# Adapter and gate weights beside base_w in one split moving operand, with products of 264 and 384 columns a tile

## What is computed

```
# L0 condition: a 32x32 channel mixer per sample, from 8 attended kernels
att = softmax(gelu(gelu(cond @ W0 + b0) @ W1 + b1) @ W2 + b2)
y   = einsum('boi,bih->boh', einsum('bk,koi->boi', att, weight), x) + (att @ bias_k)[..., None]
# L0 ffn: base layer, and the best 2 of 8 experts of rank 16
w    = top-2 softmax over e of (y @ gate_w.T)
x1   = x + y @ base_w.T + base_b + 2 * sum_e w_e * (y @ lora_A[e].T) @ lora_B[e].T
# L1: a 9-tap grouped convolution over h plus a context, then the best 2 of 4 experts
z    = conv1d(x1, 9 taps, 4 groups) + cond @ c_weight.T + fside
out  = x1 + 4 * (top-2 softmax of z @ router_w.T) over e of (z @ A[e].T) @ B[e].T
```

## Time and profile before

| what | value |
|---|---|
| three runs, median | 185.46 us |
| the profiled execution | 185.67 us |
| its span | 183.7 us |
| PE busy | 176.0 us (96%) |
| PEld busy | 160.1 us (87%) |
| DVE busy | 119.6 us (65%) |
| POOL busy | 84.2 us (46%) |
| ACT busy | 82.9 us (45%) |
| share of the chain that ended last | PE 76%, DVE 16%, ACT 4%, issue 2% |

### The profile page before, as it was taken

One profiled execution on the slowest core, in us unless ns is written; L12 is line 12 of the kernel. 1 busy time (PEld: TensorE's weight loads), 2 busy tenths in 40 slices (PEclk: granted clock), 3 DMA queues, 4 the chain that ended last, 5 costly groups with the idle time before them and its releaser, 6 DMA issues.

```text
span 183.7 us, 3003 instructions
## 1 busy us (share of the span) xinstructions
PE 176.0 (96%) x1087; PEld 160.1 (87%) x1087; DVE 119.6 (65%) x255; ACT 82.9 (45%) x183; POOL 84.2 (46%) x86
## 2 busy tenths in 40 slices
PE   7999999899999999999999999999999999988990
PEld 7998889788888999998889999988889999987970
DVE  1269795987996343987954336987756733577473
ACT  3656759538336066423442267316134652244010
POOL 8023609980396469930009099530007873433000
PEclk9999999999999999999999999999999999999999
DMA  5999000033000410000032000000140000000336
GB/s 176 312 373 366 11 0 2 4 109 121 0 0 25 149 60 0 4 0 0 0 133 99 0 2 0 4 0 0 61 167 4 2 0 4 0 0 2 114 114 228
DMA packets 6350, 12.15 MB, mean 66 GB/s; under 512 B 704, under 2 KB 1088, under 8 KB 6336
## 3 DMA queue, kind: packets, MB, share of 16 engines
q1 hardware_dynamic: 6192, 11.84, 18.1%
q10 hardware_dynamic: 144, 0.13, 0.3%
HBM read 7.77 MB, written 4.19 MB: 65 GB/s over the span
## 4 chain that ended last, share of the span: by engine, by line
PE 76%; DVE 16%; ACT 4%; issue 2%; DVEq 0%; POOL 0%; POOLq 0%
PE ps L895 17%; PE ps L897 17%; PE ps L896 17%; PE ps L917 6%; PE ps L971 5%; PE ps L888 3%; DVE xs L732 2%; DVE late L642 2%; DVE xsl L634 2%; PE ps L932 2%; DVE above L638 1%; PE ps L968 1%; PE ps L1060 1%; DVE outb L720 1%; PE ps L1079 1%
## 5 line engine op out<-in xcount | busy, mean ns | idle before, releaser
L895 PE MATMUL ps<-base_h,xTh 128*128 128x512 f32 x64 | 26.0, 406 | 0.0
L897 PE MATMUL ps<-base_h,xTl 128*128 128x512 f32 x64 | 25.2, 394 | 0.0
L896 PE MATMUL ps<-base_l,xTh 128*128 128x512 f32 x64 | 25.2, 394 | 0.0
L320 POOL TENSOR_TENSOR xTl<-xT_s,xTh 128x512 fp32r<-128x512 f32 x12 | 15.0, 1278 | 15.9 <-ACT xTh L404 15.9
L325 POOL TENSOR_TENSOR zl<-outb,zh 128x340 fp32r<-128x340 f32 x15 | 14.6, 976 | 13.4 <-ACT zh L429 13.3
L336 POOL TENSOR_TENSOR x1Tl<-x1T,x1Th 128x512 fp32r<-128x512 f32 x12 | 16.4, 1379 | 8.1 <-DVE lw L662 8.1
L691 DVE TENSOR_TENSOR outb<-ps,s_sb 128x340 f32<-128x340 f32 x16 | 8.2, 511 | 17.6 <-PE ps L897 11.2
L678 DVE SCALAR_TENSOR_TENSOR x1T<-ps,side_s,xT_s 128x512 f32<-128x512 f32 x16 | 12.0, 749 | 11.3 <-PE ps L897 11.3
L971 PEld LDWEIGHTS ps<-mixT,p 128*128 128x128 f32 x128 | 17.0, 191 | 1.4
L971 PE MATMUL ps<-mixT,p 128*128 128x128 f32 x128 | 17.0, 276 | 0.0
L429 ACT ACTIVATE zh<-outb 128x340 fp32r<-128x340 f32 x16 | 7.8, 489 | 17.9 <-DVE outb L691 13.2
(11 more groups left out here) (183 smaller groups left out, 471.5 us busy)
## 6 DMA issues: line engine op xcount, KB each, us to landing
xT_s<-in_xT_dram SPq DMA_DIRECT2D x16, 256.0 KB, 3.8
out_dram<-outb SPq DMA_DIRECT2D x16, 256.0 KB, 2.3
x1T<-in_wT_dram SPq DMA_DIRECT2D x4, 256.0 KB, 6.0
x1T<-in_az_dram SPq DMA_DIRECT2D x1, 680.0 KB, 8.3
...
```

The lines of the kernel that those rows point to most:

```text
L320: nc.gpsimd.tensor_tensor(xTl[:, c, :], xT_s[:, g % 2, c, :], xTh[:, c, :].bitcast(F32), ALU.subtract).then_inc(x_lo, 1)
L895: nc.tensor.matmul(dst, sh, mh, start=start and c == 0, stop=False)
L896: nc.tensor.matmul(dst, sh, ml, start=False, stop=False)
L897: last = nc.tensor.matmul(dst, sl, mh, start=False, stop=stop and c == n - 1)
```

## The change

The weights of lora_A and the gate (136 columns, `LG`) and of base_w (512) now stand side by side in one operand of 648 columns (`WX`), split in `xw_h` and `xw_l`. Group 0 is computed as before (float32 for the 136, split for the 512). From group 1 on, a tile's 648 columns are made by split products alone, in two passes into the same bank `P0[t]`: `x_first` makes the first 264 (`HX`: the 136 and 128 of base_w), ACT's new `xa_out` copies them out, and then `x_base` makes the other 384, which `p0_out` copies. The float32 `x_logits` of groups 1 to 3 are gone. x's high and low parts are therefore needed sooner; group 0's now lie in `x1Th` and `x1Tl`, so that group 1's in `xTh` and `xTl` can be made while group 0's are still read. The new weights' split is one ACT copy and one DVE subtraction of 544 elements, in the start-up. On PE the order within a group is changed too, and on DVE `mwT_low` now stands ahead of `logits`. Many operations carry a new line number: 921 to 923 for `hi_lo`, 950 for `mix_logits`, 428 for `xa_out`, 435 and 437 for `p0_out`, 461 for `lwT_high`, 657 for DVE's subtractions.

```diff
 LG = ER0 + E0
+WX = LG + D
+HX = LG + P
...
+
+        xw_h = sb("xw_h", [P, DC, WX], F32R)
+        xw_l = sb("xw_l", [P, DC, WX], F32R)
+        base_h, base_l = xw_h[:, :, LG:WX], xw_l[:, :, LG:WX]
...
+
+        def x_parts(g):
+            return (xTh, xTl) if g else (x1Th, x1Tl)
 
...
             shifted_low(1, sw_l[:, :, :], az_s[:, 1, :, :], sw_h[:, :, :])
             pool.wait_ge(lb_lo, 1)
+            for c in range(DC):
+                x_low(1, c)
             pool.wait_ge(dif_ok, 1)
             shifted_low(2, uw_l[:, :, :], ue[:, :, :], uw_h[:, :, :])
             pool.wait_ge(dif_ok, 2)
             shifted_low(3, vw_l[:, :, :], ud, vw_h[:, :, :])
             bias_rows(1)
-            for c in range(DC):
-                x_low(1, c)
             pool.wait_ge(tap_hi, 1)
             nc.gpsimd.tensor_tensor(tap_l[:, :, :].rearrange("p k c -> p (k c)"), tapw_s,
 
             def x_high(g, c):
                 act.wait_ge(xT_in[g % 2][c], 16 * (g // 2 + 1))
-                if g and c == 0:
+                if g > 1 and c == 0:
                     act.wait_ge(p0_mm, TG * g)
...
+
+
+            def xa_out(g, t):
+                act.wait_ge(xa_mm, TG * (g - 1) + t + 1)
+                if t == 0:
                     act.wait_ge(lw_ok, g)
-                nc.scalar.activation(lgs[:, 2 * half:2 * half + 2, :].rearrange("p t e -> p (t e)"),
-                                     ps[:, XLG[half], 0:2 * LG], ACT.Copy).then_inc(xl_ok, 1)
+                    act.wait_ge(y_mm, DC * (g - 1) + 1)
+                nc.scalar.activation(xp[:, t, 0:HX], ps[:, P0[t], 0:HX], ACT.Copy).then_inc(xa_ok, 1)
 
             def p0_out(g, t):
                 act.wait_ge(p0_mm, TG * g + t + 1)
-                if g == 0 and t == 0:
-                    act.wait_ge(agg_ok, 1)
-                nc.scalar.activation(p0[:, t, :], ps[:, P0[t], :], ACT.Copy).then_inc(p0_ok, 1)
+                if g == 0:
+                    if t == 0:
+                        act.wait_ge(agg_ok, 1)
+                    nc.scalar.activation(p0[:, t, :], ps[:, P0[t], :], ACT.Copy).then_inc(p0_ok, 1)
+                else:
+                    nc.scalar.activation(xp[:, t, HX:WX], ps[:, P0[t], 0:WX - HX], ACT.Copy).then_inc(p0_ok, 1)
 
...
             base_high(2)
             base_high(3)
-            xl_out(0, 1)
+            xl_out(1)
...
             act.wait_ge(bsum_mm, 1)
             nc.scalar.activation(row_w[:, :], ps[:, BSUM, :], ACT.Copy).then_inc(bsum_hi, 1)
+            for c in range(DC):
+                x_high(1, c)
             act.wait_ge(in_tap, 16)
             nc.scalar.activation(tap_h[:, :, :].rearrange("p k c -> p (k c)"), tapw_s, ACT.Copy).then_inc(tap_hi, 1)
             act.wait_ge(in_b1, 16)
             nc.scalar.activation(b1_h[:, :], b1T_s, ACT.Copy).then_inc(b1_hi, 1)
+            lwT_high(0)
             for t in range(TG):
                 p0_out(0, t)
-            lwT_high(0)
-            for c in range(DC):
-                x_high(1, c)
-            xl_out(1, 0)
-            xl_out(1, 1)
             for g in range(1, G):
                 mix_place(g)
+            for t in range(TG):
+                xa_out(1, t)
             bias_high(1)
                 sums_high(i, 1)
-                xl_out(n, 0)
+                xa_out(n, 0)
                 sums_high(i, 2)
-                xl_out(n, 1)
+                xa_out(n, 1)
                 sums_high(i, 3)
                 gate_exp(p, gate1, dif1_ok, ex1_ok)
+                xa_out(n, 2)
+                xa_out(n, 3)
                 p0_out(n, 0)
                 mwT_high(p)
+                gate_exp(n, gate0, dif0_ok, ex0_ok)
                 p0_out(n, 1)
                 bias_high(n)
-                gate_exp(n, gate0, dif0_ok, ex0_ok)
                 p0_out(n, 2)
...
+            minus(xw_l[:, :, 0:LG], lgw_s[:, :, :], xw_h[:, :, 0:LG]).then_inc(lgw_lo, 1)
             for t in range(TG):
...
                 route1(p)
+                mwT_low(p)
                 for t in range(TG):
                     logits(n, t)
-                mwT_low(p)
                 route0(n)
...
                 if tiles[-1]:
                     last.then_inc(xl_mm, 1)
 
             def mix_logits(i, t):
-                pe.wait_ge(xl_ok, 2 * i + t // 2 + 1)
-                if i < 2:
-                    pe.wait_ge(mix_ok, BT * (i + 1))
+                if i == 0:
+                    pe.wait_ge(xl_ok, t // 2 + 1)
                 else:
-                    pe.wait_ge(mix_ok, BT * G)
-                if i and t == 0:
-                    pe.wait_ge(lwT_lo, i)
-                elif i == 1 and t == 2:
-                    pe.wait_ge(x1_ok, DC - 1)
+                    pe.wait_ge(xa_ok, TG * (i - 1) + t + 1)
+                    if t == 0:
+                        pe.wait_ge(lwT_lo, i)
+                    elif t == 2:
+                        pe.wait_ge(x1_ok, DC * (i - 1) + DC - 1)
 
-            def x_base(g, t, chunks=range(DC)):
+
+            def x_first(g, t, chunks=range(DC)):
+                if chunks[0] == 0:
+                    if g == 1:
+                        pe.wait_ge(p0_ok, t + 1)
+                        pe.wait_ge(lgw_lo, 1)
+                    elif t == 0:
+                        pe.wait_ge(zo_ok, TG * (g - 1) - 1)
+                    elif t == 1:
+                        pe.wait_ge(s_ok, TG * (g - 1))
+                    elif t == 2:
+                        pe.wait_ge(ze_ok, TG * (g - 1))
+                    else:
+                        pe.wait_ge(zo_ok, TG * (g - 1))
+                hi, lo = x_parts(g)
                 for c in chunks:
                     pe.wait_ge(x_lo, DC * g + c + 1)
+                    last = hi_lo(ps[:, P0[t], 0:HX], [(hi[:, c, cols(t)], lo[:, c, cols(t)])],
+                                 [(xw_h[:, c, 0:HX], xw_l[:, c, 0:HX])], start=c == 0, stop=c == DC - 1)
+                if chunks[-1] == DC - 1:
+                    last.then_inc(xa_mm, 1)
+
+
+            def x_base(g, t, chunks=range(DC)):
+                first = HX if g else LG
+                hi, lo = x_parts(g)
+                for c in chunks:
                     if g == 0:
+                        pe.wait_ge(x_lo, c + 1)
                         pe.wait_ge(base_lo, c + 1)
-                    if g == 1 and c == 0:
-                        pe.wait_ge(p0_ok, t + 1)
-                    elif g > 1 and c == 0:
-                        if t == 0:
-                            pe.wait_ge(ze_ok, TG * (g - 1))
-                            pe.wait_ge(zo_ok, TG * (g - 1))
-                    last = hi_lo(ps[:, P0[t], :], [(xTh[:, c, cols(t)], xTl[:, c, cols(t)])],
-                                 [(base_h[:, c, :], base_l[:, c, :])], start=c == 0, stop=c == DC - 1)
+                    elif c == 0:
+                        pe.wait_ge(xa_ok, TG * (g - 1) + t + 1)
+                    last = hi_lo(ps[:, P0[t], 0:WX - first], [(hi[:, c, cols(t)], lo[:, c, cols(t)])],
+                                 [(xw_h[:, c, first:WX], xw_l[:, c, first:WX])], start=c == 0, stop=c == DC - 1)
                 if chunks[-1] == DC - 1:
...
                     x_base(0, t, (c,))
             turn_lw(0)
-            x_logits(1, 0)
-            pe.wait_ge(bsum_lo, 1)
-            x_logits(1, 1)
+            for c in range(DC):
+                for t in range(TG):
+                    x_first(1, t, (c,))
             make_y(0)
+            for t in range(TG):
+                mix_logits(1, t)
             pe.wait_ge(in_az, 16)
             pe.wait_ge(prod_ok, MIX_STEPS[G - 1])
             for m in range(2):
@@ -1123,34 +1167,31 @@
                     last = nc.tensor.matmul(psum_b, ones[:, :], az_s[:, m, h, 2 * PJ:3 * PJ],
                                             start=m + h == 0, stop=m + h == 2)
             last.then_inc(pjsum_mm, 1)
-            for t in range(TG):
-                mix_logits(1, t)
             x_base(1, 0)
             x_base(1, 1)
             x_base(1, 2)
-            x_base(1, 3, (0, 1))
             turn_lw(1)
-            x_base(1, 3, (2, 3))
+            x_base(1, 3)
             for i in range(1, G - 1):
                 p, n = i - 1, i + 1
                 make_y(i)
                 for t in range(TG):
                     project(p, t)
-                x_logits(n, 0)
-                x_logits(n, 1)
+                x_first(n, 0)
+                x_first(n, 1)
                 taps(p)
+                x_first(n, 2)
+                x_first(n, 3)
+                x_base(n, 0)
+                turn_mw(p)
                 for t in range(TG):
                     mix_logits(n, t)
-                x_base(n, 0)
-                x_base(n, 1, (0, 1))
-                turn_mw(p)
-                x_base(n, 1, (2, 3))
-                x_base(n, 2)
+                x_base(n, 1)
                 for c in range(DC):
                     experts1(p, c)
-                x_base(n, 3, (0, 1))
+                x_base(n, 2)
                 turn_lw(n)
```

(45 more changed lines are left out.)

28 lines of the change are left out of this document (16 added, 12 removed).

## The result

| | before | changed |
|---|---|---|
| median of 6 runs | 185.65 us (184.99 to 186.57) | 190.75 us (189.59 to 191.36) |
| profiled execution, its span | 185.67, 183.7 | 190.82, 189.1 |
| mean granted clock of that execution | 1.000 | 0.988 |

The changed kernel is slower: its time over that of before is 1.0281 [1.0242, 1.032]. Forecast were +2.7 us and 188.2, with a range up to 190.7; it came to +5.1. Where an execution lay more than 1.5% above the fastest of its kernel, the ratios of this document leave it out and the medians keep it, so the two need not agree to the last digit.

A forecast was written before the change was run, and what follows sets the result against it. PE bounds the kernel, except from 29 to 57 us, where ACT's and DVE's list is almost as long. Hand-over loss 4.03 less stage gains 1.3 gave +2.7 us: 185.46 to 188.2 us, own range 187.3 to 189.2, full range 185.3 to 190.7.

The forecast's parts named there:

- PE's prices: Split products on PE: 0.00045 us a column, so 264 columns cost 0.1214 us and 384 cost 0.1755, second weight loads nothing.
- the forecast's saving: Groups 2 and 3 on PE: 0.52 us from narrower products plus 0.18 from dropped float32-to-split changes, 0.70 a stage.
- the first group and the hand-over: Group 1's first pass waits for ACT's copies, `make_y(0)` 3.2 us later; then `lw` of group 1 4.0 us later.
- the third wait: PE in `make_y(1)`, after the mixer products, stands 3.2 us for `lwTl` from DVE.
- The restart: PE going on in `make_y(1)` once `lwTl` is there: 60.2 us instead of 56.2.
- my third rival: The 3.2 us wait lowers PE's clock: 1.5 us lost for 3 us of it; 189.7 to 192.5, middle 190.7; chance 0.10.
- the stages' gain: Two later stages, behind PE's restart: 0.70 - 0.05 us gained in each, 1.3 us together.
- `experts1`'s last product meets `p0_out(n, 1)`, which stands behind the gate's exponential, within 0.1 us: Later stages: PE's last `experts1` product and ACT's copy nearly coincide; the gain a stage is taken as 0.70 - 0.05 us.

The follow-up runs named there:

- `p0_out` first: Changed kernel with the four `p0_out(0, t)` copies ahead of `lwT_high(0)` on ACT; 188.96 us, ratio 1.0247 to the kernel before.
- exponential late: Changed kernel with only `p0_out(n, 1)` ahead of the gate's exponential on ACT in the two later stages; 188.77 us, ratio 1.0176 to the kernel before.
- mixer halves early: Changed kernel with both `mix_half(3)` ahead of `make_x1(0, 0)` on DVE; 187.64 us, ratio 1.0142 to the kernel before.
- before with a wait: Kernel before with eight extra DVE subtractions, read by nobody, ahead of `lwT_low(1)`; 189.55 us, ratio 1.021 to the kernel before.
- the other five reordered or kept busy: Changed kernel with idle-filling products 188.57 us; `lwT_low(1)` earlier 187.42; three reorderings 186.66; five moves 183.81; all moves, mixer halves one by one, 182.76.

## Why the prediction was wrong

**Right: PE's prices.** 264 columns start every (81.74 - 78.84)/24 = 0.121 us and 384 every (90.15 - 88.04)/12 = 0.176; forecast 0.1214 and 0.1755. With the stall gone each stage gains 0.7, the forecast's saving, so the 48 more weight loads cost nothing that shows. The rule of the Trainium skill (TensorE: Matmul & The Clock Gate, The mechanism in Part 3), by which they would overlap a running product only where row groups differ, isn't borne out here. The same section of the Trainium skill also lets a load into a background weight buffer go ahead of running products; starts 0.121 us apart with a load for each agree with that, and the prediction did not weigh it.

**Right in mechanism: the first group and the hand-over.** `make_y(0)` came at 37.26 (37.1), `bias_high(1)` at 46.01 (45.66), `lw` at 53.06 (52.69), `lwTl` at 60.48 (60.17), and the third wait was 3.08 us (3.2). The restart moved by 4.24 on the common zero (4.03). Of the 0.2 half lies ahead of `make_y(0)`, half between it and the restart.

**Wrong: the clock.** This is the step that failed by most: the sum has no term for the clock, and 1.6 us was lost to it. It was put at nothing, and my third rival given a chance of 0.10, on one row: the clock stayed 1.00 over 4.4 us of rest at the end. That row ended too soon. The record of the clock goes on behind the span, and in the same trace it fell at 183.9 us, 4.5 us behind PE's last product and 0.2 us behind the end of the span. A later window of before:

```profile
184.00:186.00 2.00, 0.00 (x0) 0.00 (x0) 0.00 (x0) 0.00 (x0) 0.00 (x0) 0.51 0.03 8
```

In all twelve traces the clock fell behind PE's last product, 2.2 to 5.3 us after its end, in eight of them still inside the span (the changed kernel's last window shows 0.88). So the 1.00 of the row is right, but it does not show that such a rest leaves the clock alone: the fall came just behind it, as it came behind the restart in the changed kernel.

In the middle of the kernel the fall came in 11 of the 12 executions of the changed kernel, if a mean clock of 0.991 or less is taken for it. Sorted by PE's longest rest between `turn_lw(0)` and the first `project`, as one trace of each kernel has it:

| longest rest there | executions | mean clock 0.991 or less |
|---|---|---|
| 3.1 us (changed, `p0_out` first, exponential late) | 20 | 18 |
| 2.8 to 2.9 us (mixer halves early, before with a wait) | 10 | 6 |
| 1.6 us or less (the other five reordered or kept busy) | 30 | 0 |
| 0.5 us (before, as it ran beside the experiments) | 35 | 1 |

The mean says that there was a fall, not where, and takes in the one at the end (up to 2.1 us of the span in these traces, which alone gives 0.994). In the three traces of 0.988, 0.986 and 0.991 a fall lay behind this wait; in the three others that have such a wait (3.08, 2.88 and 2.77 us, mean clocks 0.994, 0.998 and 1.000) none did. It cost 1.6 us (3.4 us at half pace); the rival had 1.5 for 3 us, so its size was right, and with it the forecast would have been 189.8. That the rival's middle, 190.7, is the time measured is luck: it stands for a longer fall than there was, and the rest came from the stages. By the Trainium skill (TensorE: Matmul & The Clock Gate, Why this matters for your kernels) gaps between bursts drop the clock; by that rule this was the case, and the runs agree: 18 of 20 behind 3.1 us, and 6 of 10 behind 2.8 to 2.9.

**Wrong: the stages' gain.** The term of 1.3 us for both was 0.5. The step that failed is "`experts1`'s last product meets `p0_out(n, 1)`, which stands behind the gate's exponential, within 0.1 us", priced at 0.05 a stage: it cost 0.44 (39.21 - 38.77). PE wanted the bank at 94.80 (94.57 + 0.23) and the copy ended at 95.09, since the exponential came only at 94.34. The prediction does not work out when it would come. Two lists within 0.1 us of each other are a coin's toss, and a miss costs more than its overlap: the pause's end has its own price.

**The sum.** 4.24 + 1.60 - 0.51 = +5.3 us, against +2.7: 1.6 from the clock, 0.8 from the stages, 0.2 from the hand-over. The medians differ by 5.1 us, so nothing over 0.2 us is left without a cause.

**Left open.** Why 2.8 us of rest kept the clock in four executions of ten and 3.1 us in two of twenty isn't settled. That DVE's list behind `lw_ok` is long because of POOL was not tried: no run moved POOL's work away. The changed kernel's trace speaks for it: DVE's subtraction `xsl<-xs,xsh` of 256 columns took 1.52 us at 54.75 and 1.48 at 57.61, with POOL at work from 53.14 to 58.81, and the same subtraction took 0.42 us at 84.79 and at 85.36, with POOL idle from 83.73 to 85.87.
